# A flag of its own for the first tile's weights at the begin of the second expert layer

## The reference, cut to what matters

```python
def _L1_ffn_ref(x, gate_w, w1, w2):
    K = 2
    xt = x.reshape(-1, D)                       # 2048 tokens, D = 256
    logits = jnp.einsum('td,ed->te', xt, gate_w)    # E = 8 experts
    w_topk, sel = jax.lax.top_k(logits, K)
    w_topk = jax.nn.softmax(w_topk.astype(jnp.float32), axis=-1).astype(x.dtype)
    combine = jnp.zeros((T, E), dtype=x.dtype)
    combine = combine.at[jnp.arange(T)[:, None], sel].add(w_topk)
    h = jax.nn.silu(jnp.einsum('td,edf->tef', xt, w1))      # 256 -> 1024
    y = jnp.einsum('tef,efd->ted', h, w2)                   # 1024 -> 256
    out = jnp.einsum('ted,te->td', y, combine)
    return out.reshape(x.shape)

x = x + jnp.tanh(g_xattn[0]) * _L0_xattn_ref(_layernorm(x), ctx_1024, ctx_1024)
x = x + jnp.tanh(g_ffn[0]) * _L0_ffn_ref(_layernorm(x), Wg, W_in, W_out)
x = x + jnp.tanh(g_xattn[1]) * _L1_xattn_ref(_layernorm(x), ctx_1024, ctx_1024, Wq, bq, Wk, bk, Wv, bv, mask, 1)
x = x + jnp.tanh(g_ffn[1]) * _L1_ffn_ref(_layernorm(x), gate_w, w1, w2)
```

## Time and profile before

| What | Value |
|---|---|
| median of three runs | 600.43 us (598.79 to 601.91) |
| the profiled execution's own time | 598.61 us |
| its span, first to last instruction | 596.8 us |
| TensorE busy | 533.6 us (89%) |
| VectorE / ScalarE / GpSimd busy | 328.0 / 309.4 / 224.6 us |
| mean granted TensorE clock | 0.932 |

### The profile page before, as it was taken

The page is one execution under the profiler, slowest core; times in us unless marked ns, Lnnn a source line. Parts: engine busy times, 40 slices in busy tenths (PEclk is TensorE's granted clock), DMA queues, the critical chain, the costliest instruction groups (busy, mean ns, idle before and its releaser), DMA issues.

```text
span 596.8 us, 12258 instructions
## 1 busy us (share of the span) xinstructions
PE 533.6 (89%) x3599; PEld 483.7 (81%) x3604; DVE 328.0 (55%) x804; ACT 309.4 (52%) x666; POOL 224.6 (38%) x258
## 2 busy tenths in 40 slices
PE   3798889999999999998981599999999999999991
PEld 1577879999999999977761388989898989898981
DVE  1878825755566656375879624453535453454430
ACT  3665335756575664435777135564545463455530
POOL 2400574455446541241000324544444544453531
PEclk9686599999999999799995599999999999999996
DMA  7954152454345452540144054444444444442221
GB/s 253 366 188 142 54 164 85 143 183 134 110 153 181 140 162 90 170 149 0 37 142 107 27 169 106 107 113 113 108 106 106 108 112 114 102 110 35 43 39 19
DMA packets 51727, 71.43 MB, mean 120 GB/s; under 512 B 7057, under 2 KB 43409, under 8 KB 51697
## 3 DMA queue, kind: packets, MB, share of 16 engines
q1 hardware_dynamic: 40752, 50.31, 26.2%
q0 software_dynamic: 10944, 20.76, 16.1%
HBM read 50.72 MB, written 20.33 MB: 119 GB/s over the span
## 4 chain that ended last, share of the span: by engine, by line
PE 72%; DVE 14%; issue 4%; DMA 2%; ACT 2%; SPq 1%; DVEq 1%; ACTq 0%; POOL 0%; POOLq 0%
PE PA L1572 25%; PE PD L1572 22%; PE PC L1572 8%; PE PC L1775 4%; PE PB L1429 3%; DVE stats L928 2%; PE PB L1584 2%; PE PD L1429 2%; DVE ys L1066 2%; PE PC L1429 2%; DVE wlo L1186 1%; DMA xs<-x 1%; PE PA L1429 1%; PE PB L1757 1%; DVE xs L1235 1%
## 5 line engine op out<-in xcount | busy, mean ns | idle before, releaser
L1572 PE MATMUL PD<-whi,hhi 128*128 128x256 f32 x420 | 122.8, 292 | 0.3 <-DVEq L1370 0.3
L1572 PE MATMUL PD<-wlo,hhi 128*128 128x256 f32 x420 | 118.6, 282 | 0.0
L1572 PE MATMUL PD<-whi,hlo 128*128 128x256 f32 x420 | 118.6, 282 | 0.0
L567 POOL DMA_INDIRECT out<-ys,row_o x35 | 55.8, 1595 | 106.7 <-DVE ys L1380 106.4
L1572 PEld LDWEIGHTS PD<-whi,hhi 128*128 128x128 f32 x420 | 79.9, 190 | 1.0 <-DVEq L1370 0.5
L1572 PEld LDWEIGHTS PD<-wlo,hhi 128*128 128x128 f32 x420 | 80.2, 191 | 0.0
L1572 PEld LDWEIGHTS PD<-whi,hlo 128*128 128x128 f32 x420 | 80.1, 191 | 0.0
L886 ACT ACTIVATE hhi<-PC 128x512 fp32r<-128x512 f32 x70 | 38.1, 595 | 68.1 <-PE PC L1775 66.1
L485 POOL DMA_INDIRECT xg<-xn_rows,row_x x45 | 45.0, 1000 | 66.0 <-DVEq L1052 39.6
L881 ACT ACTIVATE xT<-PA 128x512 f32<-128x512 f32 x72 | 42.2, 599 | 49.8 <-PE PA L1572 49.6
L492 POOL DMA_INDIRECT y_rows<-ys,row_y x40 | 41.8, 1046 | 61.0 <-ACT ys L713 59.5
(11 more groups left out here) (258 smaller groups left out, 1256.5 us busy)
## 6 DMA issues: line engine op xcount, KB each, us to landing
raw<-w SPq DMA_DIRECT2D x16, 1024.0 KB, 5.7
raw<-L_ffn_W_in SPq DMA_DIRECT2D x8, 1024.0 KB, 5.1
raw<-L_ffn_W_out SPq DMA_DIRECT2D x8, 512.0 KB, 3.6
y_rows<-ys SPq DMA_DIRECT2D x8, 512.0 KB, 7.2
xn_rows<-xn SPq DMA_DIRECT2D x8, 512.0 KB, 3.3
xs<-x SPq DMA_DIRECT2D x4, 512.0 KB, 7.8
cx<-ctx SPq DMA_DIRECT2D x4, 512.0 KB, 8.5
ys<-y_rows SPq DMA_DIRECT2D x4, 512.0 KB, 4.3
```

The source lines that it names most:

```text
L567: pool.indirect_dma_start(out, bass.IndirectOffsetOnAxis(ap=row_o[:, j:j + 1], axis=0), ys[:, j % 2, :], None, compute_op=ALU.add).then_in ...
L1572: mm = pe.matmul(dst, a[k], b[k], start=(first and k == 0 and a is lhs_hi and b is rhs_hi), stop=(last and k == n - 1 and a is lhs_lo))
```

## The change

A new 128x1 tile `first_i` is computed from `te` right behind line 1314, 32 where expert 0 has no tile and 0 elsewhere, and has a semaphore of its own, `first_ready`. ACT and DVE each read it into a register in place of `landed(0)`. The first two steps of the table (lines 1328 and 1329) move ahead of `turned_slots(1)`. On DVE the read of the flag stands between the four semaphore raises and the rest of the table; `xt1(0,0)` moves ahead of `win1(0)`, and `number` moves behind `win1(1)`. On ACT `win1(0)` and `xt1(1,1)` move ahead of the wait for `tab_ready`.

```diff
+        first_i = sb("first_i", [P, 1], I32)
...
+        first_ready = sem("first_ready")
...
+        def first_of(engine):
+
+            return engine.value_load(first_i[0:1, 0:1], min_val=0, max_val=32)
...
             act.sem_inc(silu_done, 2)
+            act.wait_ge(first_ready, 1)
+            first = first_of(act)
             xt1(0, 0)
+            win1(0, first)
+            xt1(1, 1)
             act.wait_ge(tab_ready, 1)
             needed = number(act)
-            win1(0, landed(0))
-            xt1(1, 1)
             silu1(0)
             win1(1, landed(1))
...
             link(dve.tensor_scalar(te[:, 3, :], te[:, 2, :], float(P), None, ALU.mult))
+            dve.tensor_scalar(first_i[:, :], te[:, 0, 0:1], 0.0, 32.0, ALU.is_equal, ALU.mult).then_inc(first_ready, 1)
             dve.wait_ge(rank_done, 2)
             pick(te[:, 3, :])
             coefs(3, NQ - 1)
             maps(1, smi[:, 2, :])
+            over_a = c("iota_a").unsqueeze(2).broadcast_to([P, NA, E])
+            ends, starts = (te[:, n, :].unsqueeze(1).broadcast_to([P, NA, E]) for n in (1, 2))
+            link(dve.tensor_tensor(tab, over_a, ends, ALU.is_ge))
+            link(dve.tensor_reduce(tabf[:, 0, :], tab, AX.X, ALU.add))
             turned_slots(1)
             dve.sem_inc(xt1_lo, 2)
             dve.sem_inc(ht1_lo, 2)
             dve.sem_inc(y1_evac, 2)
             dve.sem_inc(ys1_free, 2)
-            over_a = c("iota_a").unsqueeze(2).broadcast_to([P, NA, E])
-            ends, starts = (te[:, n, :].unsqueeze(1).broadcast_to([P, NA, E]) for n in (1, 2))
-            link(dve.tensor_tensor(tab, over_a, ends, ALU.is_ge))
-            link(dve.tensor_reduce(tabf[:, 0, :], tab, AX.X, ALU.add))
+            dve.wait_ge(first_ready, 1)
+            first = first_of(dve)
             link(dve.tensor_scalar(tabi[:, TAB_EXPERT, :], tabf[:, 0, :], float(E - 1), None, ALU.min))
...
-            needed = number(dve)
-            win1(0, landed(0))
             xt1(0, 0)
+            win1(0, first)
             xt1(1, 1)
             targets()
             split1(0, wout_hi[1], wout_lo[1], piece_out)
             win1(1, landed(1))
+            needed = number(dve)
             step(0, 0, last=False)
```

## The result

The changed kernel takes 599.0 us in the median of 22 runs (596.33 to 601.42), the one before 601.03 in 22 runs beside them (598.59 to 603.35). The ratio is 0.9962, 95% interval 0.995 to 0.9975: 2.3 us faster, between 1.5 and 3.0. The prediction said 598.7, a gain of 1.7.

A forecast was written before the change was run, and what follows sets the result against it. TensorE's matmul train bounds the layer, its head held by 2.42 us from tab_ready to hid1. The table nets +0.02; reads and branch leaving that way give 1.70 off 600.43: 598.7 us, range 597.3 to 599.9, with rivals 596.6 to 600.7.

The forecast's parts named there:

- The flag: Added 128x1 VectorE instruction behind line 1314, on the chain: everything up to the maps' end 0.10 us later (0.05 to 0.20).
- The two steps: Table steps of 1.05 us fit VectorE's 1.07 idle beside the last map matmuls; row numbers at most 0.1 late, 0.02 taken.
- The read inside the table: VectorE's flag read, as its first load, costs 0.95 us (other end 0.63); tab_ready comes 0.02 later in sum.
- Behind tab_ready: Two register reads and a branch leave the way to tile 0's split; first hid1 matmul 1.70 us earlier.
- The next bound: Tile 1's transposes on TensorE, ending 0.4 us ahead of hid1's new start; no faster table could gain over 2.1.
- Nothing gives it back: Behind the head, win1(1), the moved number, tile 2's gather and ACT's chain all keep up, so the 1.70 us stays.
- Rival 1: TensorE's clock at the head rises where it rose, or later: gain only 1.4 or 0.4, 599.2 to 600.0 us; chance 0.22.
- Rival 2: TensorE's clock rises earlier as the idle gap before hid1 shrinks: 2.0 us more, gain 3.7, 596.7 us; chance 0.09.
- the low stretch: TensorE's half-speed clock behind the first hid1 matmul, taken to last 3.9 us as before.
- Rival 3: VectorE's flag read waits for flushes, or the table steps don't fit: each costs up to 1.0, 600.0 us; chance 0.08.
- Rival 4: Slower: TensorE's clock stays low over the first tiles, up to 13.5 us, losing 4.8, 603.5 us; chance 0.03.

The follow-up runs named there:

- e2: Changed kernel with the two table steps back behind VectorE's flag read; first te step to first hid1 matmul 19.48 us, ratio to the kernel before 0.9987.
- e3: Changed kernel with VectorE's flag read moved ahead of the two table steps, right behind the maps; ratio to the kernel before 0.9934.
- e6: Changed kernel with VectorE's flag read done twice in the same place; first te step to first hid1 matmul 19.05 us.
- e11: Kernel before, unchanged, profiled a second time; first te step to first hid1 matmul 20.13 us, from there to the first out1 matmul 10.16.
- e12: Changed kernel, unaltered, profiled a second time; first te step to first hid1 matmul 18.42 us, from there to the first out1 matmul 9.07.
- e4: Changed kernel with 8 unused 128x128 matmuls added behind the map matmuls; ratio to the kernel before 0.9972.
- e10: e3 with 12 unused matmuls behind the map matmuls and 3 between the transposes of tiles 0 and 1; ratio to the kernel before 0.9941.
- e5: Kernel before with 8 unused 128x128 matmuls added behind the map matmuls; ratio to the kernel before 1.0017.

## Why the prediction was right

That nothing changes beyond 0.5%, the direction and the size hold. That the time itself is off by only 0.3 is partly luck: the kernel before is 601.03 in 22 runs and not 600.43, 0.60 more, and the two medians lie 2.03 apart and not 1.7, so the two errors partly cancel. By steps:

- **The flag**: 0.10 taken, 0.07 measured. The Trainium skill ("VectorE: DVE Perf Modes", The DRAIN you can't avoid) says that leaving out the semaphore saves nothing, by which it would have cost the linked step's 0.20; for this unwaited 128x1 operation the trace does not agree. With the flag, the copy came 0.13 later where 0.12 was expected: e2 puts 0.06 on the flag and leaves 0.07 for the move.
- **The two steps**: their cover held, with 0.23 of idle time left where the prediction had 0.02. e2 measures 1.08 on the head, 1.09 on the table. The 0.07 that they cost the row numbers (0.02 taken) is the hand-over's and not a missing cover's.
- **The read inside the table**: 0.95 taken; in the trace it stands from 334.19 to 335.12, 0.93; e3 finds 0.90 on the table when it leaves, e6 adds 0.65 for another. So the table stood still, at 17.52 in both: 0.13 for the copy, 0.93 for the read, 1.05 off for the two steps.
- **Behind tab_ready**: 2.42 became 0.69; the prediction had 0.7. Head 1.73 shorter, 1.70 forecast.
- **The next bound** was mis-sized: the prediction had hid1 wait for the listed end of tile 1's transposes, so that no faster table could gain over 2.1. In e3 hid1 started 0.42 behind their start, not the listed 0.69, and the head was 2.35 shorter than before. The changed kernel didn't reach that bound, so the forecast didn't hang on it.
- **Nothing gives it back**: hlo is still released by ACT, the wait before out1 is 0.29, and from the first out1 matmul to the end it is 249.45 before and 249.12 changed (249.22 and 249.29 in e11 and e12, their second profiles).
- **Rival 1** (the clock rises where it rose, or later) fell for the changed kernel: 2.9 and 3.0 us behind hid1. **Rival 2** (it rises earlier) was partly true, though its reason, the shorter gap, isn't shown, and here is the mis-sized term: I took the low stretch as unchanged, 3.9 us. The profiles show 3.9 and 5.6 before, 2.9 and 3.0 changed, which is worth 0.78 us of TensorE's train. 1.73 + 0.78 = 2.5 is the profiles' gain; the runs say 2.3 (1.5 to 3.0), an interval that holds 1.73 as well, so the runs alone don't show that the clock added anything. **Rival 3** (the read costs more behind unfinished work, or the steps don't fit) fell: the read cost 0.93 where the sum had 0.95, and the steps fitted. **Rival 4** was not seen; no low stretch at the head lasted over 5.6.
- The Trainium skill ("TensorE: Matmul & The Clock Gate", What's actually happening) lets the rise fall differently from run to run. With 3.9 and 5.6 us in the same kernel, the trace agrees.

## What to carry to other kernels

Look at the sequencer between a ready signal and the engine that needs it: a further register read with its checks cost 0.65 us and the first one 0.93, more than most small vector operations here, and it was free where it stood behind long instructions already queued on its engine (e3). Where a step is moved into an idle gap, ask which work makes the gap, and whether something else could have stood in it: here the two steps and the read both fitted under the maps, in two different places. For an effect of 0.3%, anchor two profiles at a step ahead of the change; the two whole spans differed by 0.5 us in the wrong direction.

## What the runs showed of the hardware that I had not expected

- The clock can rise and be lost again within a few microseconds: in e4 it was up from about 334.9 and down by 338.4, with TensorE idle in two gaps of 1.13 and 0.78 us between. In e10, with the gaps filled, it stayed.
- The first te step, ahead of which the change and the experiments alter next to nothing, starts between 315.8 (e10) and 321.3 (e5), and on one chip still between 317.2 (e2) and 320.2 (e6).
- TensorE's next matmul can start before the listed (modelled) end of the one before: in e3 hid1 started 0.42 us behind the start of transposes listed with 0.69.
